# A two-layer gated cross-attention and FFN kernel: three bias products turned into additions in the copies out of PSUM, and all instruction streams written in a new order

## The reference

```python
x = x + tanh(g_xattn[0]) * L0_xattn(ctx, ctx, layernorm(x), Wk, bk, Wq, bq, Wv, bv, Wo, bo)   # softmax over the 16 heads
x = x + tanh(g_ffn[0])   * L0_ffn(layernorm(x))      # silu(gate) * up, 768 hidden columns, then down
x = x + tanh(g_xattn[1]) * L1_xattn(layernorm(x), ctx, Wq, Wkv, Wo)   # one key/value head, softmax over the keys
x = x + tanh(g_ffn[1])   * L1_ffn(layernorm(x))      # W + low-rank product, with a bias
```

## Time and profile before

| | before |
|---|---|
| median of 3 runs | 2888.66 us (2888.55 to 2889.1) |
| the profiled execution's own time | 2889.29 us |
| its span, first to last instruction | 2887.5 us |
| busy: PE, DVE, ACT, POOL | 97%, 86%, 55%, 50% |
| TensorE clock granted | 1.00 over the span |
| DMA | 75 MB, mean 26 GB/s |

### The profile page before, as it was taken

One profiled execution on the slowest core, in us unless ns is written; L12 is line 12 of the kernel. 1 busy time (PEld: TensorE's weight loads), 2 busy tenths in 40 slices (PEclk: granted clock), 3 DMA queues, 4 the chain that ended last, 5 costly groups with the idle time before them and its releaser, 6 DMA issues.

```text
span 2887.5 us, 80157 instructions
## 1 busy us (share of the span) xinstructions
PE 2813.6 (97%) x33173; PEld 2461.8 (85%) x33173; DVE 2486.6 (86%) x4246; ACT 1577.7 (55%) x3031; POOL 1441.1 (50%) x1633
## 2 busy tenths in 40 slices
PE   3999999999999999999999999999999999999999
PEld 2888888888888888888888888888888888888888
DVE  5888888888888888888888888888888888888888
ACT  3555555555555555555555555555555555555555
POOL 4445545544554554454455455445545544544554
PEclk9999999999999999999999999999999999999999
DMA  2000000000000000000000000000001000000000
GB/s 72 28 20 26 27 22 28 24 29 20 25 27 20 29 24 29 20 25 27 20 28 25 24 25 25 27 20 25 27 20 29 24 29 20 25 27 20 29 24 24
DMA packets 75914, 74.99 MB, mean 26 GB/s; under 512 B 6123, under 2 KB 75009, under 8 KB 75906
## 3 DMA queue, kind: packets, MB, share of 16 engines
q1 hardware_dynamic: 75906, 74.89, 8.5%
HBM read 57.30 MB, written 17.56 MB: 26 GB/s over the span
## 4 chain that ended last, share of the span: by engine, by line
PE 70%; POOL 23%; issue 3%; ACT 3%; POOLq 1%; DVE 0%; DMA 0%; SPq 0%; DVEq 0%
PE work L845 13%; PE work L716 12%; PE work L717 10%; PE work L718 10%; POOL h_lo L309 10%; POOL zt L312 8%; PE scores L799 5%; PE work L757 4%; POOL zt L316 3%; PE work L733 3%; PE scores L810 3%; PE scores L820 2%; PE work L742 2%; ACT e L418 2%; POOL zt L319 2%
## 5 line engine op out<-in xcount | busy, mean ns | idle before, releaser
L418 ACT ACTIVATE e<-scores 120x1024 f32<-120x1024 f32 x536 | 520.1, 1023 | 261.9 <-PE scores L825 251.4
L309 POOL TENSOR_TENSOR h_lo<-h_f,h_hi 128x256 fp32r<-128x256 f32 x402 | 426.3, 1073 | 204.8 <-ACT h_hi L381 201.1
L716 PE MATMUL work<-xt_hi_B,w_hi 128*128 128x256 f32 x1608 | 474.2, 295 | 10.7 <-DVE e L548 10.7
L717 PE MATMUL work<-xt_lo_B,w_hi 128*128 128x256 f32 x1608 | 454.7, 283 | 0.0
L718 PE MATMUL work<-xt_hi_B,w_lo 128*128 128x256 f32 x1608 | 454.4, 283 | 0.0
L312 POOL TENSOR_TENSOR zt<-e 120x512 f32<-120x512 f32 x268 | 342.9, 1290 | 100.4 <-ACT e L418 100.4
L601 DVE TENSOR_TENSOR e<-e,rz 120x2048 f32<-120x2048 f32 x134 | 375.5, 2802 | 2.3
L412 ACT ACTIVATE th<-work 128x256 f32<-128x256 f32 x402 | 154.4, 384 | 393.3 <-PE work L718 393.3
L588 DVE TENSOR_REDUCE m<-scores 120x128 fp32r<-120x2048 f32 x134 | 307.0, 2291 | 63.7 <-PE scores L810 63.4
L303 POOL TENSOR_TENSOR rstd_B<-var_eps_B,minus_half 128x2 f32<-128x2 f32 x67 | 46.1, 689 | 604.1 <-DVE var_eps_B L563 604.1
L716 PEld LDWEIGHTS work<-xt_hi_B,w_hi 128*128 128x128 f32 x1608 | 306.9, 191 | 29.2 <-issue 11.4
(11 more groups left out here) (194 smaller groups left out, 7689.9 us busy)
## 6 DMA issues: line engine op xcount, KB each, us to landing
x_ln<-xp SPq DMA_DIRECT2D x67, 256.0 KB, 2.8
x_res<-xp SPq DMA_DIRECT2D x67, 256.0 KB, 2.7
y<-y_out SPq DMA_DIRECT2D x67, 256.0 KB, 2.2
ctx_f_A<-cp SPq DMA_DIRECT2D x67, 128.0 KB, 2.6
ctx_f_C<-cp SPq DMA_DIRECT2D x67, 128.0 KB, 2.1
e<-wi SPq DMA_DIRECT2D x3, 768.0 KB, 5.5
e<-wf SPq DMA_DIRECT2D x2, 512.0 KB, 3.6
w_ctx<-wc SPq DMA_DIRECT2D x1, 656.0 KB
```

The source lines that it names most:

```text
L309: return pool.tensor_tensor(h_lo[:, m, :], h_f[:, m % 2, :], h_hi[:, m, :].bitcast(F32), ALU.subtract)
L418: return act.activation(e[0:SC, c, 2 * h:2 * h + 2, :, :].rearrange("p a b n -> p (a b n)"), scores[0:SC, 2 * h:2 * h + 2, :].rearrange("p ...
L716: pe.matmul(out, a_hi, b_hi_, start=first, stop=False, skip_group_check=parts)
L717: pe.matmul(out, a_hi, b_lo_, start=False, stop=False, skip_group_check=parts)
```

## The change

Three products go. The key bias is added by ScalarE and VectorE as they copy `keys0` out of PSUM (one instruction becomes two, one per 128 columns, on each engine). The query bias is added by ScalarE in `query_out("A")` (one instruction becomes two). The value bias is added by VectorE, which takes the copy `values0_out` over from ScalarE (two instructions). Before the loop, five small products on TensorE and five small instructions on VectorE put the biases where these copies need them, and VectorE clears one more bank.

All five streams are in a new order, and a pass of the loop now begins at another place of the work. `STAGES_BEHIND` is 4, so that the loop has 64 + 4 = 68 passes. The number of other instructions in a pass is the same on every engine.

```diff
-STAGES_BEHIND = 3
+STAGES_BEHIND = 4
...
             def query_out(st, bank):
-                return act.activation(qt[st][:, :], bank[:, :], ACT.Copy)
+                if st == "C":
+                    return act.activation(qt[st][:, :], bank[:, :], ACT.Copy)
+                for oc in range(KC):
+                    last = act.activation(qt[st][:, oc * S:(oc + 1) * S], bank[:, oc * S:(oc + 1) * S], ACT.Identity,
+                                          bias=bias_col[:, oc:oc + 1])
+                return last
...
             def keys0_odd(bank):
-                return dve.tensor_scalar(kz0[:, 1, :, :], bank[:, 0:KC * P].rearrange("p (k n) -> p k n", k=KC),
-                                         parity[:, 1:2], None, ALU.mult)
+                for kc in range(KC):
+                    last = dve.tensor_scalar(kz0[:, 1, kc, :], bank[:, kc * P:(kc + 1) * P], parity[:, 1:2],
+                                             key_bias[:, 1, kc:kc + 1], ALU.mult, ALU.add)
+                return last
+
+            def values0_out(bank):
+                v_src, v_add = (a[0:SC, 0:D].rearrange("p (g r j) -> p g r j", r=2, j=HD) for a in (bank, val_bias))
+                dve.tensor_tensor(v0_pad[0:SC, :, 0:HD], v_src[:, :, 0, :], v_add[:, :, 0, :], ALU.add)
+                return dve.tensor_tensor(v0_pad[0:SC, :, 48:48 + HD], v_src[:, :, 1, :], v_add[:, :, 1, :], ALU.add)
...
             def keys0(bank):
...
-                    last = pe.matmul(bank[:, oc * P:(oc + 1) * P],
-                                     bias_k[:, BIAS["k0"] + oc * P:BIAS["k0"] + (oc + 1) * P], ones_k[:, 0:P],
-                                     start=False, stop=True)
...
             def values0(bank):
...
-                return pe.matmul(bank[:, 0:D], ones_k[:, 0:P], bias_k[:, BIAS["v0"]:BIAS["v0"] + D], start=False, stop=True)
...
-                queries(W[0], "A", "q0", True)
+                queries(W[3], "A", "q0", False).then_inc(s["q_mm_A"], 1)
```

More of the change, by code:

```diff
@@ L339, in _ @@
                 heads_total(1, t).then_inc(s["A1_z"], 1)
+                pool.wait_ge(s["G_hi"], nth(4, 6, t))
+                hidden_lo(4).then_inc(s["G_lo"], 1)
+                pool.wait_ge(s["G_hi"], nth(5, 6, t))
+                hidden_lo(5).then_inc(s["G_lo"], 1)
                 pool.wait_ge(s["ln_eps_C"], t)
@@ L609, in _ @@
             with nc.vector.Fori(FIRST, last_t + 1) as t:
-                dve.wait_ge(s["A1_mm"], t - 1)
+                dve.wait_ge(s["M0_mm"], t - 1)
+                key_max(0).then_inc(s["M0_max"], 1)
+                dve.wait_ge(s["T_hi_A"], t)
+                transposed_lo("A", W[3]).then_inc(s["T_lo_A"], 1)
+                values0_out(W[2])
+                dve.wait_ge(s["T_hi_B"], t)
+                transposed_lo("B", W[0]).then_inc(s["T_lo_B"], 1)
+                dve.wait_ge(s["M1_mm"], t)
@@ new lines, in _ @@
+                key_max(1).then_inc(s["M1_max"], 1)
+                residual(x3, x2_before, W[1]).then_inc(s["res_C"], 1)
+                dve.wait_ge(s["res_C"], t)
+                moments("D", x3, t).then_inc(s["ln_eps_D"], 1)
+                dve.wait_ge(s["A0_mm"], t)
+                head_max(0).then_inc(s["A0_max"], 1)
+                dve.wait_ge(s["G_tanh"], nth(0, 6, t))
+                gated(0, W[0]).then_inc(s["G_a"], 1)
+                dve.wait_ge(s["G_a"], nth(0, 6, t))
+                hidden(0, W[0]).then_inc(s["G_h"], 1)
@@ L625, in _ @@
+                dve.wait_ge(s["G_lo"], nth(3, 6, t))
+                hidden(5, W[3]).then_inc(s["G_h"], 1)
                 dve.wait_ge(s["ld_x_ln"], 16 * t)
                 moments("A", x_ln, t)
+                dve.wait_ge(s["A1_z"], t)
+                reciprocal0(1).then_inc(s["A1_rz"], 1)
+                dve.wait_ge(s["A1_rz"], t)
+                normalise(1).then_inc(s["A1_p"], 1)
                 dve.wait_ge(s["dn_mm"], nth(5, 6, t))
@@ L630, in _ @@
                 moments("C", x2, t).then_inc(s["ln_eps_C"], 1)
-                dve.wait_ge(s["A1_z"], t)
-                reciprocal0(1).then_inc(s["A1_rz"], 1)
-                dve.wait_ge(s["A1_rz"], t)
-                normalise(1).then_inc(s["A1_p"], 1)
-                dve.wait_ge(s["kz0_even"], t)
-                keys0_odd(W[1]).then_inc(s["kz0_odd"], 1)
                 dve.wait_ge(s["zC"], t)
                 reciprocal1(0)
+                dve.wait_ge(s["yA_hi"], t)
+                low(y_lo["A"][:, :, :], two(W[3], KC), y_hi["A"][:, :, :]).then_inc(s["yA_lo"], 1)
@@ L688, in _ @@
-                hidden(3, W[0]).then_inc(s["G_h"], 1)
-                dve.wait_ge(s["f1_mm"], t)
-                dve.wait_ge(s["st_out"], 16 * (t - 1))
-                residual(y_out, x3, W[3]).then_inc(s["res_D"], 1)
+                dve.wait_ge(s["yC_hi"], t)
+                low(y_lo["C"][:, :, :], y1f[:, :].rearrange("p (k n) -> p k n", k=KC), y_hi["C"][:, :, :])\
+                    .then_inc(s["yC_lo"], 1)
         @block.tensor
@@ L934, in _ @@
-                scores0(1).then_inc(s["A1_mm"], 1)
 def kernel(**inputs):
```

433 lines of the change are left out of this document (219 added, 214 removed), and 10 rows, old and new, of the table per_pass.

## The result

The changed kernel takes 2899.85 us (median of six runs, 2899.34 to 2900.17) against 2888.64 us before: a ratio of 1.0038, with a 95% interval of 1.0025 to 1.0051. It is slower by 11 us. The forecast said slower, by 49 us, with a range of 2900 to 2990 us. The sign was right; the size was not, and the range missed by 0.15 us.

A forecast was written before the change was run, and what follows sets the result against it. TensorE, busy 97%, was taken as the bound. A pass of 42.32 us loses 0.92 and 0.66, gains 0.2 and 1.47: 42.41; 68 passes, 52.8 us of setup and end, and 1.8 give 2938 us, range 2900 to 2990.

The forecast's parts named there:

- The wait that comes in: TensorE at down(4) waits for GpSimd's hidden_lo(4): a 9.79 us chain against 8.32 us of work, 1.47 us a pass.
- Handing over at once: GpSimd starts as VectorE's blocking normalise(0) ends, as the trace shows; a 115 ns hand-over would lengthen the chain 0.26 us.
- The old wait: TensorE's wait for GpSimd's hidden_lo ahead of down(4) in the kernel before goes away, saving 0.66 us a pass.
- The borders between kinds of products: On TensorE, products of one kind behind another: two charged at 0.1 us each, bounds 0 and 0.4 us a pass.
- The bias products: Removing TensorE's key, value and query bias products saves 0.37, 0.31 and 0.24 us, together 0.92 us a pass.
- The sum of a pass without the wait: TensorE's pass of 42.32 us, less bias products and old wait, plus 0.2 us for borders: 40.94 us.
- Close waits: TensorE's waits for key_max(0) and the last copies (query_out("C"), xn_A), each within 0.2 us: 0 taken, upper bound 0.3 us.
- The rival in which VectorE becomes the bound: VectorE's slack behind A1_z is missing: 0.7 us more, 43.1 us a pass, 2985 us; chance 0.08.
- Setup: Before the loop, bias preparation and clearing PSUM on VectorE add 2.5 us (bounds 0 and 3.4) to 49.9 us.
- The end: Behind the last pass no store and no sum of block D remain: 0.4 us in place of 2.2.
- The even point: The 68-pass loop equals the old time at 41.69 us a pass, 0.63 below 42.32.
- The block is hidden: Rival: normalise(0) stays out of GpSimd's chain, so TensorE never waits: 40.94 us a pass, 2838 us, 1.7% faster; chance 0.14.

The follow-up runs named there:

- Experiments 1: Changed kernel: normalise(0) replaced by a one-SBUF-input reduction, 2797.0 us; its reciprocals kept in PSUM instead, 2797.18 us; kernel before with reciprocals in PSUM, 2842.19 us.
- experiment 2: Changed kernel: normalise(0) moved to just ahead of normalise(1), 2908.35 us; separately, hidden_lo(4) between the add_heads and hidden_lo(5) ahead of heads_total(1), 2971.77 us.

## Why the prediction was right and wrong

- **The wait that comes in: right, to its size.** 1.47 us was forecast, and 1.46 (list of waits) to 1.53 us (the pass with and without it) measured. The chain of 9.79 us on GpSimd was measured at 9.79. TensorE's work over the same stretch is 8.26 us where the sum had 8.32. Experiments 1 and 2 showed the mechanism. Handing over at once, as the rows of before had it, was the right reading. The 0.26 us more by the Trainium skill ("SBUF — State Buffer", "A bandwidth-pool intuition that's wrong") did not come; the figure there was measured on a DMA whose descriptors GpSimd writes, not on a sum of GpSimd.
- **The old wait, 0.66 us: right**; taking it out of the kernel before gave 0.69.
- **The borders between kinds of products: the step that failed.** The prediction charged 0.2 us for "about as many such borders", with 0 as the lower bound. The new order has three fewer changes of tile and gave time back: 0.76 us a pass with the bias products and 0.51 without, of which 0.55 and 0.65 us are not spacing of equal products. A gain had not been excluded by any reason; the bound at 0 was only asserted. Against the 0.2 charged that is 0.71 to 0.96 us a pass, and it alone puts a pass's lower bound of 42.1 us above the 41.88 measured.
- **A term that the sum did not have: the spacing of the fp32r products**, 0.1193 us before and 0.1179 in the new order, 0.21 us a pass. It is a part of the 0.76 above, and its cause stays open.
- **The bias products, 0.92 us: too much.** Key, query and value were taken at 0.37, 0.24 and 0.31 us. In the new order they cost 0.17, 0.22 and 0.13; in the old one, with the spacing set aside, 0.16, 0.14 and 0.12. The query's price was nearly right in the new order. The key's and the value's were not, since what follows them, of another kind, has its own distance with or without them. Part of a distance read behind a product belongs to the border.
- **The sum of a pass without the wait**: 42.29 - 0.69 - 0.76 - 0.52 = 40.32 us, measured 40.33, forecast 40.94. The two errors, +0.40 and -0.96 us, partly cancel, and together with the wait they leave 42.41 against 41.88 us: 0.53 x 68 explain 36 of the 38 us. With the border term alone put right, the forecast would have been 41.45 us a pass and the kernel faster; with the bias products put right too, it is 41.85.
- **Close waits taken at 0, and VectorE not the bound: right in the changed kernel.** TensorE's list of waits has no other in the loop; its weight loads have one of 0.3 us a pass for `xn_A`, which the forecast had named as close. The rival in which VectorE becomes the bound did not come; experiment 2 showed how near it is.
- **Setup: 3.7 us too long.** The first product of the loop was forecast at 52.4 us and came at 48.67. The traces say why. The inputs landed at 6.95 us in place of 8.08; in the other kernels they landed between 6.83 and 8.10, so that this is scatter, and the 49.91 us of before a late case (the same setup gave 48.86 in the run with the reciprocals in PSUM). The added instructions cost 1.2 us in place of 2.5 (0.67 for the biases, 0.54 for the bank). And one instruction of VectorE became 1.19 us shorter: GpSimd no longer clears `h_lo` beside it. Two rows of before, then one of the change:

```profile
39.93 1.68 DVE L537 TENSOR_SCALAR e<-e,tg 128x512 f32<-128x512 f32 x1
...
39.95 1.38 POOL L299 MEMSET h_lo<- 128x1536 f32 x1
```

```profile
39.34 0.49 DVE L554 TENSOR_SCALAR e<-e,tg 128x512 f32<-128x512 f32 x1
```

The first product follows the inputs by 41.8 us before and by 41.7 in the change. The end was 1.1 us in place of 0.4.

- **The even point: right.** It was forecast at 41.69 us a pass; with the setup measured it is 41.73. The pass of 41.88 us misses it by 0.15, times 68: 10 us slower. The sign therefore hung on 0.15 us a pass, not on the 0.7 us that the forecast gave, and the 0.81 for slower were too sure. That the sign came out right is in part luck, since it needed two errors of opposite sign.
- **"The block is hidden" (0.14)** priced a pass without the wait at 40.94 us and 2838 us; such a kernel, made by experiment, has 40.33 us and 2797 us.

## What to carry to other kernels

Before an order of TensorE's work is priced, count how often the tile changes (17 and 14 here) and give that term both signs; a border is a cost that moves with its neighbours, not with the product in front. When two runs differ, look where in the pass the difference lies before it is put down to the edit: over half of what the key's and the query's bias products seemed to cost in the old order lay in products that the edit did not touch. Where a VectorE sum of two SBUF operands meets GpSimd on the critical path, try an operand in PSUM: here it was worth 103 us after and 46 us before, more than the change under study. An instruction of 0.28 us costs what stands ahead of it in its queue.

## What the runs showed of the hardware

- A VectorE instruction with two SBUF inputs of 120x2048 and GpSimd's sums exclude each other for their whole length (4.59 us for two sums in place of 2.53); with one input in PSUM they don't (2.28 us beside 2.53), and a reduce with one SBUF input of 3.86 us doesn't block either. The Trainium skill ("SBUF — State Buffer", "Who interferes with whom") has the same rule, and the trace agrees.
- A VectorE `tensor_scalar` of 128x512 from SBUF to SBUF took 1.68 us in the seven kernels in which GpSimd cleared a tile in SBUF beside it (1.38 us), and 0.49 us in the ten in which it did not.
- A change of tile on TensorE costs about 0.12 us: 0.09 us more from the last of four transposes to scores on 32 rows, 0.11 us more behind the scores, 0.23 us for two changes by experiment. Going from float32 to fp32r on the whole array costs 0.03 us.
- The value product cost 0.12 to 0.13 us when taken out or put back, where its distance in the trace of before is 0.31 us.
- The same fp32r product of 256 columns follows the one ahead of it in 0.1170, 0.1179 or 0.1193 us on average, by the kernel; the cause is open.
